# Queries of two cross attentions projected as three fp32r products of split tokens and weights

## What is computed

```python
Q = (q @ Wq + bq).reshape(Bc, Tq, H, HD).transpose(0, 2, 1, 3)
KV = (kv @ Wkv + bkv).reshape(Bc, Tk, 2, H, HD).transpose(2, 0, 3, 1, 4)
attn = jnp.einsum('bhqd,bhkd->bhqk', Q, K) * scale   # layer 0: masked keys are -inf
out = jnp.einsum('bhqk,bhkd->bhqd', softmax(attn), V)
return out.transpose(0, 2, 1, 3).reshape(Bc, Tq, Dm) @ Wo + bo
```

## Time and profile before

| | |
|---|---|
| time, median of 3 runs | 3012.79 us |
| profiled execution: its time | 3016.17 us |
| its span, first to last instruction | 3014.4 us |
| TensorE busy | 2643.4 us (88%) |
| VectorE busy | 1692.8 us (56%) |
| GpSimd busy | 1566.5 us (52%) |
| ScalarE busy | 1175.0 us (39%) |
| mean granted TensorE clock | 0.941 of full |
| first cross attention (c0) | 1779 to 2042 us, clock 0.94 |
| second cross attention (c1) | 2573 to 2848 us, clock 0.91 |

### The profile page before, as it was taken

The page is one execution under the profiler, slowest core; times in us unless marked ns, Lnnn a source line. Parts: engine busy times, 40 slices in busy tenths (PEclk is TensorE's granted clock), DMA queues, the critical chain, the costliest instruction groups (busy, mean ns, idle before and its releaser), DMA issues. The chain is left out here.

```text
span 3014.4 us, 42642 instructions
## 1 busy us (share of the span) xinstructions
PE 2643.4 (88%) x11953; PEld 1606.9 (53%) x11953; DVE 1692.8 (56%) x3340; ACT 1175.0 (39%) x1644; POOL 1566.5 (52%) x1299
## 2 busy tenths in 40 slices
PE   5999999999999999999999968883696588788696
PEld 4666666666666666666666533432474244443254
DVE  4566665666656666565665634663234555468743
ACT  2444444444444444444444324451122334344234
POOL 0677666776767766676676741223433313222343
PEclk8999999999999999999999989996898599899798
DMA  7545555454555546455454320003894100000233
GB/s 188 119 101 122 114 129 112 106 119 109 122 113 118 115 103 134 106 122 120 98 121 113 77 70 21 2 2 112 322 333 157 48 0 1 30 2 9 55 117 89
DMA packets 406654, 305.26 MB, mean 101 GB/s; under 512 B 291830, under 2 KB 337182, under 8 KB 401438
## 3 DMA queue, kind: packets, MB, share of 16 engines
q1 hardware_dynamic: 390702, 233.93, 33.2%
q0 software_dynamic: 11904, 64.06, 6.0%
q10 hardware_dynamic: 3952, 6.08, 0.6%
HBM read 190.18 MB, written 96.49 MB: 95 GB/s over the span
## 5 line engine op out<-in xcount | busy, mean ns | idle before, releaser
L630 POOL TENSOR_TENSOR a_total<-a_total,a_pr 128x1024 f32<-128x1024 f32 x384 | 915.1, 2383 | 56.5 <-ACT a_pr L614 36.2
L561 DVE TENSOR_REDUCE a_nmax<-a_psX 128x1 f32<-128x512 f32 x1024 | 696.0, 688 | 167.5 <-PE a_psX L556 165.6
L614 ACT ACTIVATE a_pr<-a_psS 128x1024 f32<-128x1024 f32 x512 | 524.9, 1026 | 676.5 <-PE a_psS L602 676.5
L642 PE MATMUL a_psO<-a_pr,a_vd 128*64 128x512 f32 x2048 | 481.8, 602 | 0.0
L556 PE MATMUL a_psX<-a_kA,a_qA 128*128 128x512 f32 x1024 | 411.3, 403 | 29.3 <-DVE a_pl L458 16.5
L630 POOL TENSOR_TENSOR a_total<-a_pr 128x1024 f32<-128x1024 f32 x64 | 153.4, 2396 | 520.1 <-ACT a_pr L614 520.1
L602 PE MATMUL a_psS<-a_qA,a_kA 128*128 128x512 f32 x1024 | 338.4, 412 | 1.6 <-DVE a_nT L577 1.4
L602 PE MATMUL a_psS<-a_qB,a_kB 128*128 128x512 f32 x1024 | 320.5, 394 | 0.7 <-DVE a_qB L585 0.7
L642 PEld LDWEIGHTS a_psO<-a_pr,a_vd 128*64 128x64 f32 x2048 | 129.9, 136 | 236.4 <-issue 179.3
L556 PEld LDWEIGHTS a_psX<-a_kA,a_qA 128*128 128x128 f32 x1024 | 193.0, 189 | 106.9 <-issue 32.0
L602 PEld LDWEIGHTS a_psS<-a_qA,a_kA 128*128 128x128 f32 x1024 | 180.9, 189 | 121.8 <-issue 90.1
(11 more groups left out here) (388 smaller groups left out, 4336.3 us busy)
## 6 DMA issues: line engine op xcount, KB each, us to landing
a_qA<-a_qhi SPq DMA_DIRECT2D x128, 256.0 KB
a_qhi<-a_ph SPq DMA_DIRECT2D x128, 128.0 KB, 2.1
a_qlo<-a_pl SPq DMA_DIRECT2D x128, 128.0 KB, 2.2
a_khi<-a_ph SPq DMA_DIRECT2D x128, 128.0 KB, 3.1
a_klo<-a_pl SPq DMA_DIRECT2D x128, 128.0 KB, 3.0
a_kA<-a_khi SPq DMA_DIRECT2D x64, 256.0 KB
a_kA<-a_klo SPq DMA_DIRECT2D x64, 256.0 KB
a_kB<-a_khi SPq DMA_DIRECT2D x64, 256.0 KB
```

The lines of the kernel that those rows point to most:

```text
L561: w.eng.tensor_reduce(nmax[:, half, u:u + 1], psX[:, half, :], AX.X, ALU.max, negate=True)\
L614: w.eng.activation(pr[:, n, :], psS[:, half, :, :].rearrange("p a b -> p (a b)"), ACT.Exp, scale=SCALE)\
L630: w.eng.tensor_tensor(total[:, buf, :], first, pr[:, n, :], ALU.add).then_inc(sems["ad"], 1)
L642: last = w.eng.matmul(psO[q * HD:(q + 1) * HD, :], vd[:, b, kc, :], pr[:, n, q * 512:(q + 1) * 512], start=kc == 0, stop=kc == KC - 1)
```

## The change

The tokens and the query weights are each split in two fp32r parts, the rounded value (h) and what the rounding leaves (l). queries multiplies wqh by xh, wql by xh and wqh by xl, each in two products over the 256 channels: six fp32r products of 128x512 in place of two fp32 ones. ScalarE makes xh beside xT, from the same bank, and GpSimd makes xl = xT - xh. The weights are split once per stage. cx lies in xT's place, wq and wk in oT's.

```diff
@@ cross_attention
-        wq, wk = (m.sb(n, [P, 2, NQ * P]) for n in ("wq", "wk"))
+        wqh, wql = (m.sb(n, [P, 2, NQ * P], F32R) for n in ("wqh", "wql"))
...
-        cx = m.sb("cx", [TK, B, D])
...
         xT = m.sb("xT", [P, 2, BT])
+        xh, xl = (m.sb(n, [P, 2, BT], F32R) for n in ("xh", "xl"))
+        cx = xT[0:TK, :, :].rearrange("p a b -> p (a b)").rearrange("p (b c) -> p b c", c=D)
...
         oT = m.sb("oT", [P, 2, 2, BT])
+        wq, wk = oT[:, 0, :, :], oT[:, 1, :, :]
...
+        def split_weights(w):
+            if w.on("scalar"):
+                w.wait("wq", 16)
+                w.eng.activation(wqh[:, :, :], wq, ACT.Copy).then_inc(sems["wh"], 1)
+            if w.on("gpsimd"):
+                w.wait("wh", 1)
+                w.eng.tensor_tensor(wql[:, :, :], wq, wqh[:, :, :].bitcast(F32), ALU.subtract).then_inc(sems["wl"], 1)
@@ turn_x
+            cols = slice(half * 256, (half + 1) * 256)
             if w.on("scalar"):
                 w.wait("mi", w.at("mi"))
-                w.eng.activation(xT[:, :, half * 256:(half + 1) * 256], psM[:, k, :].rearrange("p (a b) -> p a b", a=2), ACT.Copy)\
-                    .then_inc(sems[f"m{k}"], 1)
+                w.wait("xl", w.at("xl"))
+                w.eng.activation(xT[:, :, cols], psM[:, k, :].rearrange("p (a b) -> p a b", a=2), ACT.Copy).then_inc(sems["xh"], 1)
+                w.eng.activation(xh[:, :, cols], psM[:, k, :].rearrange("p (a b) -> p a b", a=2), ACT.Copy).then_inc(sems[f"m{k}"], 1)
+            w.inc("xh")
             w.inc(f"m{k}")
-            came["x", half] = (f"m{k}", w.at(f"m{k}"))
+            if w.on("gpsimd"):
+                w.wait("xh", w.at("xh"))
+                w.wait(f"m{k}", w.at(f"m{k}"))
+                w.eng.tensor_tensor(xl[:, :, cols], xT[:, :, cols], xh[:, :, cols].bitcast(F32), ALU.subtract).then_inc(sems["xl"], 1)
+            w.inc("xl")
@@ queries
             if w.on("tensor"):
-                w.wait("wq", 16)
-                for half in range(2):
-                    w.wait(*came["x", half])
+                w.wait("wl", 1)
+                w.wait("xl", w.at("xl"))
                 w.wait(f"m{k}", w.at(f"m{k}"))
-                for cc in range(2):
-                    last = w.eng.matmul(psM[:, k, :], wq[:, cc, c * P:(c + 1) * P], xT[:, cc, :], start=cc == 0, stop=cc == 1)
+                for i, (wp, xp) in enumerate(((wqh, xh), (wql, xh), (wqh, xl))):
+                    for cc in range(2):
+                        last = w.eng.matmul(psM[:, k, :], wp[:, cc, c * P:(c + 1) * P], xp[:, cc, :],
+                                            start=i == 0 and cc == 0, stop=i == 2 and cc == 1)
@@ walk
             for cc in range(2):
                 turn_context(w, cc)
+            split_weights(w)
             keys(w)
```

More of the change, by code:

```diff
@@ L909, in cross_attention @@
         psM = m.ps("psM", [P, RB, 512])
-        names = ("cst", "cstv", "x", "cx", "wk", "wq", "wv", "wo", "mi", "m0", "m1", "m2", "k", "kf", "kb", "qr", "qm", "s",
+        names = ("cst", "cstv", "x", "cx", "wk", "wq", "wv", "wo", "wh", "wl", "xh", "xl", "mi", "m0", "m1", "m2", "k", "kf", "kb", "qr", "qm", "s",
                  "ex", "pv", "tk", "dv", "ot", "xb", "var", "pl", "rstd", "y")
@@ L1345, in _ @@
         def _(eng):
-            eng.dma_start(cx[:, :, :], kv.rearrange("b k c -> k b c")).then_inc(sems["cx"], 16)
-            eng.dma_start(wk[:, :, :], w_k.rearrange("(a p) o -> p a o", p=P)).then_inc(sems["wk"], 16)
+            eng.dma_start(cx, kv.rearrange("b k c -> k b c")).then_inc(sems["cx"], 16)
+            eng.dma_start(wk, w_k.rearrange("(a p) o -> p a o", p=P)).then_inc(sems["wk"], 16)
             if y is not None:
@@ L1397, in _ @@
                 eng.dma_start(mraw[:, :], mask.partition_broadcast(P)).then_inc(sems["wk"], 16)
-            eng.dma_start(wq[:, :, :], w_q.rearrange("(a p) o -> p a o", p=P)).then_inc(sems["wq"], 16)
+            eng.dma_start(wq, w_q.rearrange("(a p) o -> p a o", p=P)).then_inc(sems["wq"], 16)
             eng.dma_start(wo[:, :, :], w_o.rearrange("(a p) o -> p a o", p=P)).then_inc(sems["wo"], 16)
```

## The result

The changed kernel takes **3060.03 us** (median of 4 runs, 3056.70 to 3062.18) against 3012.09 (4 runs, 3010.98 to 3013.42) of the kernel before: ratio 1.0156 [1.0140, 1.0172], **48 us slower**. The profiled execution took 3062.18 us.

A forecast was written before the change was run, and what follows sets the result against it. TensorE's list of instructions was taken as the bound. Blocks n = 1 to 5, n = 0 and starts (10 x 1.0 + 2 x 0.4 + 5.8 = 16.6) plus 26 for the clock gave +43: 3056 us, range 3025 to 3082.

The forecast's parts named there:

- The products: Each queries call: six fp32r products take 1.37 us against 1.72, saving 0.35, or 1.4 per block of four calls.
- The slip in a steady block: Blocks n = 1 to 5: queries(0) starts 2.4 us later, net +1.0 us in each of the 10 blocks.
- the three links named: Before queries(0): 0.6 us ScalarE's wait for xl(0) behind rstd, 0.54 for xh(1), 1.27 for xl(1).
- The DMA wait ahead of scores: Next block's scores may wait a few tenths for a DMA, covered by the 1.04 us wait at 1968.04.
- Block n = 0: No rstd ahead of xl(0): slip 1.8 us, net +0.4, twice; clock loss counted half, 2.4 in all.
- The start: Each stage's start: queries begins 3.8 us later, net +2.9 per stage, +5.8; clock adds 2.4 in each.
- the weights' split lies under the keys: Stage start: splitting the query weights lies under the key projection, 1788.61 to 1795.5, and costs nothing.
- The clock: TensorE drops to 1.2 GHz after the 2.7 us pause: 2.4 us in eight of 10 blocks, 19; 26 with starts and n = 0.
- a stage clock near 0.8: Granted clock of the two stages falls from 0.94 and 0.91 to about 0.8.
- Clock holds: Rival: TensorE keeps its clock through the new pause; +16.6, 3029 us; chance 0.15.
- Longer losses: Rival: each pause costs 3.8 us less 0.3, in every block; +66, 3079 us; chance 0.12.
- Split is hidden: Rival: xl(1) ends by 1947.3, queries(0) doesn't wait, the 22 us come in whole; 2991 us; chance 0.05.

The follow-up runs named there:

- e8: The change with useless fp32r products written to free bank psS in the pause, 10 in blocks n = 0 to 5 and 17 per start, all waits kept; ratio 1.0062.
- e3: The change with queries back to two fp32 products, while the split, its copies, subtractions and waits stay; ratio 1.0275.
- e4: e3 with queries waiting only for xT and xh, not xl, and ScalarE's wait before the xT copy one turn back; ratio 1.0038.
- e5: The change with queries(0) moved behind scores 2 and two of the largest steps, and ScalarE's wait one turn back; ratio 1.0004.
- e12: e5 with block 0's turns between the key projection's halves, and a denser order in layer 0's blocks 0 to 5 and layer 1's 0 to 2; 0.9941, 2992.4 us.
- e1: The change with useless fp32r products in the pause, 11 per block and 18 per start, written to the bank queries overwrites; ratio 1.0126.
- e2: The change with ScalarE's wait before the xT copy put back by one turn, to the xl before; ratio 1.0107.
- e6: The change with xl made by VectorE straight from the bank and no xT copy, for blocks n > 0; ratio 1.0034, 3028 us.

## Why the prediction was right

3056 was predicted and 3060.0 measured; for the two stages together +43 and +43.5. The mechanism held, and e8, e3 and e4 show its parts: the wait, the clock behind it and the saving of the products. That the sum comes out so close is in part luck: the blocks cost 32.2 us where 29 was predicted, the starts with block n = 0 11.3 where 13.8 was. By its steps:

- **The products.** 0.35 us a call was predicted. Two calls now span 2.98 us against 3.52, 0.27 a call, 1.1 a block; the blocks with the clock held give 2.43 - 1.14 = 1.3. The row of self attention, whose six products stand in front of something else, was a little too short a price.
- **The slip in a steady block.** 2.4 predicted, 2.76 - 0.32 = 2.44 measured, by the three links named: xl(0) behind rstd, xh(1), xl(1). The subtraction was taken at 1.27 and has a median of 1.276. Net +1.0 predicted, +1.14 measured in e8 in a steady block. Over all ten blocks e8 is 12.9 us longer than before, against the 10 predicted: block n = 5 of c1, which the prediction took for a steady one, is 1.9 us longer, and 1.7 even in e4, where nothing on TensorE waits for xl. The prediction's sum leaves that out. The DMA wait ahead of scores (0.31) came out of the wait for oT (1.04 before, 0.66 now), as said.
- **Block n = 0.** Waits of 2.12 and 2.03 us for xl, before of 0.40 and 0.30 for xT: 1.7 each, where 1.8 of slip was predicted. The clock stayed behind the first (a pair of products takes 0.63 us) and fell behind the second (1.05), so counting it for half fits.
- **The start.** A wait of 4.8 us for a predicted slip of 3.8 against a wait of 0.94 before: right. First outputs came 6.0 and 5.3 us later (77.6 and 73.2 us after the stage's start), 11.3 where the slip, block 0 and the clock make 2 x (2.9 + 0.4 + 1.2 + 2.4) = 13.8. Of the 6.0, 0.8 stand ahead of the transposes of X, with the landing of the loads. How the rest divides is open: e8, which fills both pauses, needed 70.3 and 72.3 us, less than before in one stage and more in the other, and the landing of the loads moves the start as well. That the weights' split lies under the keys held.
- **The clock.** 19 us predicted in the ten blocks, 19.3 measured (the change against e8). The total hit, its parts did not: I had 2.4 us in eight of ten blocks; it was 1.1 to 1.3 us in five of them, 2.0 to 2.7 in four and 3.5 in one. Two errors met. All ten lost something, and half of them lost little: in the one that I looked at the clock was back before the scores (behind the wait that ends at 1907.14, two pairs of query products take 1.05 and then the scores 1.10). I expected a stage clock near 0.8; it is 0.89 and 0.85.
- **The rivals.** "Clock holds" (3029) was e8's case, 3038 against a before of 3020, and needs the pause filled. "Longer losses" is what the fp32 products would have paid (e3, 4.0 a block). "Split is hidden" is true only once other work stands in the pause (e5, e12). The rule of a tolerated gap of about 3 us in the Trainium skill, "TensorE: Matmul & The Clock Gate", section "Why this matters for your kernels", would have given 16 to 17 us for the change. The trace doesn't agree: this kernel lost clock in all ten blocks behind pauses of 2.67 to 2.76 us.

## What to carry to other kernels

A cheaper product saves only its own microseconds; a wait that its preparation puts on the bounding engine costs its length, and then the clock behind it, so price both, and read what stands ahead of the new instruction on the helper's queue (here four tiny rstd instructions and an in-order copy). Where such a chain can't be shortened, move independent work into the pause: the same arithmetic went from 1.6% slower to 0.6% faster by its order and one wait put back by a turn. Do it only in the blocks where the engine that reads that work has room.

## What the runs showed that was not expected

- Behind pauses of the same length the clock went different ways: after 1.30 us eleven products took 4.35 or 2.78 us (e1), in three of ten blocks the former; after 1.97 to 2.06 us nine of ten blocks lost some (e2); after 2.67 to 2.76 all ten did. Yet in block n = 0 of the change a wait of 2.12 us (c0) kept the clock and one of 2.03 us (c1) lost it, and in e2 both kept it (pairs of products of 0.63 us behind them). The length of a pause alone doesn't decide it. What else does was not found.
- Ten useless products per block (and 17 per start) made a kernel 0.9% faster, because they held the clock (1.00 in every block, 28.9 us a steady block against 30.0 to 31.6).
- In c1 block n = 5, where VectorE also chooses tokens, every kernel with the split needs 1.7 us or more beyond before (30.33): 32.0 in e4 and e6, 32.3 in e8, 32.4 in e5, 34.3 in the change. In e4, e5, e6 and e8 TensorE waits 1.3 to 1.4 us there for VectorE's maxima, which it doesn't in the kernel before. Why they come later was not looked into.
- The price of a lost clock depends on what stands behind it: 1.1 to 2.7 us in most blocks with fp32r queries, 4.0 with fp32 ones.
